# Layers 0 and 1 as one list of steps with two gates, and a new layout of layer 0's tensors

## Chip, cores and metric

The kernel runs on one core of a Trainium2 chip. The metric is the device time of one execution in microseconds (us); the median of a few runs is compared. Engines are named as in the profile: PE is TensorE (PEld its weight loads), DVE is VectorE, ACT is ScalarE, POOL is GpSimd, SP is SyncE, which here only issues DMAs.

## Reference

Four attention layers follow one another on 8 batches. Cut to the two that the change touches (layers 2 and 3, a grouped-query attention and an attention with a feed-forward part, fill the span from about 1400 us on):

```python
# layer 0: x [8,256,512], ctx [8,256,512], 16 heads of 16 channels, tokens along the last axis
q, k, v = Wq x + bq, Wk ctx + bk, Wv ctx + bv
attn = softmax(where(mask, (q/4)^T k, -inf))          # per head 512 x 512
mean, ex2 = attn v, attn v^2
std = sqrt(relu(ex2 - mean^2))
x = (instance_norm(x, mask) * std + mean) * mask
# layer 1: latents = x (256 of 512), 256 rows of ctx before them as keys, 16 heads of 32
h = concat(ctx, latents)                               # 512 tokens
q, k, v = latents q_w + q_b, h kv_w + kv_b
a = softmax(where(mask, q k^T / 32, -inf)) v
a = rmsnorm(a out_w + out_b + latents)
x = gelu(a mlp_w1 + mlp_b1) mlp_w2 + mlp_b2 + latents
```

Layer 1's batch b needs layer 0's output of batch b alone, which goes through a DRAM scratch (`x1`).

## The kernel before

Work is cut into 16 items: batch b and half h (8 heads each), item i = 2b + h. Each item goes through a chain of steps with names like `("0.smax", b, h, j)`. Each engine is given one list of steps and works through it strictly in that order; steps wait for each other through semaphores (`q.wait_ge(...)`). The lists come from the functions `layer0_order` to `layer3_order`, which give each step a position in beats: a position of 17.4 means that the step belongs 0.4 of a beat into beat 17. A beat is one item's time. Positions set the order alone: what a beat lasts comes out of the run. `order_of` (line 225) sorts each engine's list by position plus a small engine-dependent delay from `LATER` (line 211).

Layer 0, for item i: beat i+1 holds projections (`proj`), the split of q and k into three bf16 parts on ACT, DVE and POOL (`split`), their way through DRAM into stacked operands QS and KS (`stack`, SP), and `v`. Beat i+2 holds 32 score matmuls with a row maximum each on DVE (`smax`, L722 on PE and L1260 on DVE), then `rows` and `turn`, which write the negative maxima as further operand rows. Beat i+3 (from 0.25 on, reaching 0.64 into the next) holds 32 score matmuls (`sc`, L731) with an exponential on ACT each (L1050), `vals` (L741, the product with v), `fold` on POOL (L1563), `sums` (L749) and the copies `out` and `sout`. Beat i+4 holds the reciprocals of the sums (`fetch`, `inv`, `spread`, through DRAM) and for h = 1 the tail of the batch: `f1`, `f2`, `f3`, `f3b`, `sq`, `f4`, `f5`, of which the last stores x1.

Layer 1, for item i, positions from i on: `load` (latents and ctx^T, DMAs from POOL), the mask row (L1304, L1307, then `mrow` by SP into KX), `lat` (transposes, L617), `kproj` and `qproj` (2 each), `v` (4), `smax` (4 steps of 4 heads, PE L781 and L784, DVE L1319), `rows`, `turn`, `sc`, `vals`, `fold`, `sums`, and for h = 1 the output projection.

PSUM: ring A (banks 0 to 2) takes projections, v, layer 0's smax and turn; ring C (3 to 5) layer 0's sc; bank 6 vals; bank 7 layer 0's sums. Layer 1's smax and sc share one group, banks 3, 4, 5 and 7 (`GROUP`): each step refills all four as they are emptied.

The two layers meet as follows. `pipeline` (line 35) ends layer 0 with a barrier at beat 19. At a barrier all five engines wait until everything before it is done (DMAs counted up to a mark at 18). Then comes `1.start`: ACT issues the DMAs of four weights of 1024 KB each, SP two bias rows, POOL memsets KX, M3 and the ones. Then the tail of item 15 (fetch to f5) runs beside `load`, `lat`, `kproj`, `qproj` and `v` of layer 1's item 0. A second barrier follows, and after it `smax` of item 0 and the rest of layers 1, 2 and 3 in one sorted list. The barriers are there because the layers' tensors lie on the same SBUF addresses. From the second barrier on no all-engine barrier stands until the end; later overlaps are guarded by "gates" (`GATED`, line 235), at which only the engines named wait until what precedes a "mark" is done.

Of the kernel before, what the change touches and what calls it, by code (L numbers as in the profile page):

```python
# [16 lines left out]


def merge(*lists):

    placed = []
    for n, (steps, start, end) in enumerate(lists):
        for i, s in enumerate(steps):
            if s is not None and isinstance(s[0], float):
                placed.append((start + (end - start) * s[0], n, i, s[1]))
                continue
            s, delay = s if isinstance(s, tuple) and isinstance(s[1], float) else (s, 0.0)
            placed.append((start + (end - start) * (i + 0.5) / len(steps) + delay, n, i, s))
    return [(at, s) for at, _, _, s in sorted(placed, key=lambda x: x[:3]) if s is not None]


SPANS = ((0.0, 0.9), (0.0, 0.8), (0.05, 0.8), (0.0, 1.0), (0.0, 1.0))


def pipeline(stages, spans=SPANS, tail=None, keep=False, begin=()):


    n, order = len(ITEMS), []
    first = 0 if stages[0] else 1
    for i in range(first, n + 4):  # L40
        lists = []
        for s, (f, span) in enumerate(zip(stages, spans)):
            if f and 0 <= i - s < n:
                steps = f(*ITEMS[i - s])
                if steps:
                    lists.append((steps, *span))
        if i == n + 3 and keep:
            return order + [(i, ("barrier", 0, 0, 0))], lists[0]
        if i == n + 2 and keep:
            order.append((i, ("mark", -1, 0, 0)))  # L50
        if i == first and tail:
            order += [(i + at, st) for at, st in merge(*lists, (tail[0], 0.0, 0.8))]
            order += [(i + 1, ("barrier", 0, 0, 0))] + [(i + 1, st) for st in begin]
        else:
            order += [(i + at, st) for at, st in merge(*lists)]
    return order + [(n + 4, ("barrier", 0, 0, 0))], None
# [1911 lines left out]
```

## Time and profile before

| | |
|---|---|
| median of 3 runs | 3267.26 us (3261.61 to 3276.46) |
| profiled execution | 3280.75 us, span 3279.0 us |
| mean granted PE clock, profiled execution | 0.92 of full speed |
| busy share of the span: PE / DVE / ACT / POOL | 86% / 56% / 41% / 27% |
| layer 0 | start to about 690 us |
| weights and first projections of layer 1 | 690 to 747 us |
| layer 1, rest | 747 to about 1400 us |

In the rows below, times are us from the start of the span. The profile's page first shows busy time by engine, then the span in 40 slices of 82 us with the busy share in tenths. A row of the timeline has start, duration, engine, line, operation, output and inputs, and how many instructions were merged; in brackets stands how long the engine was idle before it and what ended that. "Landing" of a DMA is the time from its issue to its last byte.

### The profile page before, as it was taken

Reading aid. Unit: us, or ns where it says so; the run is one execution under the profiler, and the core shown is the slowest. Engines: PE = TensorE matmul, PEld = TensorE weight load, DVE = VectorE, ACT = ScalarE, POOL = GpSimd, SP = SyncE. Lnnn points to the kernel's source line nnn. Section 1 sums busy time; section 2 is a strip of 40 time slices with the busy share of each in tenths; the row PEclk is TensorE's granted clock in tenths of the full one; section 3 lists DMA queues with packets and bytes.
Section 4 is the critical chain, followed back from the end, with each engine's and each line's share of the span. In section 5 each row is a group of like instructions: output and inputs, shape, how many; then the busy total and the mean of one; then the engine's idle time right before and its main releaser. Section 6 shows DMA issues by size and latency. Waiting matters only on the chain. (4 is left out here: it accounts for less than half of the span.)

```text
span 3279.0 us, 41359 instructions
## 1 busy us (share of the span) xinstructions
PE 2819.3 (86%) x14624; PEld 1322.2 (40%) x14624; DVE 1838.1 (56%) x4498; ACT 1339.5 (41%) x2342; POOL 882.9 (27%) x722
## 2 busy tenths in 40 slices
PE   4999998858999999989999999986678888888895
PEld 1222222224555555556555545542223333233332
DVE  3777777713444433212555565567867676667641
ACT  0566666632333333322334333322215544554562
POOL 1677777742444444310010001001111010100000
PEclk7999999979999999899999999987678899999997
DMA  4444444220002000121323332333333232323210
GB/s 99 102 103 103 109 100 102 62 94 33 27 27 83 27 28 24 66 79 42 68 59 62 63 65 55 68 63 88 66 91 80 67 78 58 90 58 71 69 32 20
DMA packets 182335, 219.93 MB, mean 67 GB/s; under 512 B 40840, under 2 KB 135664, under 8 KB 175984
## 3 DMA queue, kind: packets, MB, share of 16 engines
q1 hardware_dynamic: 170064, 189.74, 25.2%
q0 software_dynamic: 6016, 20.98, 1.9%
q10 hardware_dynamic: 6048, 6.56, 0.6%
q8 instruction: 116, 1.90, 0.3%
q14 instruction: 91, 0.75, 0.1%
HBM read 146.90 MB, written 51.64 MB: 61 GB/s over the span
## 5 line engine op out<-in xcount | busy, mean ns | idle before, releaser
L1480 DVE TENSOR_REDUCE l_M<-PS 128x1 f32<-128x512 f32 x512 | 334.4, 682 | 136.9 <-PE PS L967 134.0
L1260 DVE TENSOR_REDUCE l_M<-PS 128x1 f32<-128x512 f32 x512 | 331.8, 683 | 139.6 <-PE PS L722 138.8
L1199 ACT ACTIVATE l_P<-PS 128x512 f32<-128x512 f32 x512 | 286.3, 599 | 252.9 <-PE PS L977 235.4
L1563 POOL TENSOR_TENSOR l_S<-l_P 128x512 f32<-128x512 f32 x256 | 327.2, 1311 | 67.4 <-ACT l_P L1050 67.4
L1050 ACT ACTIVATE l_P<-PS 128x512 f32<-128x512 f32 x512 | 278.4, 598 | 103.5 <-PE PS L731 101.7
L967 PE MATMUL PS<-l_KS,l_QS 97*128 97x512 bf16 x512 | 207.9, 417 | 99.5 <-DVE l_M L1480 68.6
L1319 DVE TENSOR_REDUCE l1a_M<-PS 128x1 f32<-128x512 f32 x256 | 158.8, 681 | 203.6 <-PE PS L784 203.6
L1164 ACT ACTIVATE l_P<-l_P 128x1024 f32<-128x1024 f32 x128 | 135.3, 1057 | 301.8 <-DVE l_P L1400 301.6
L1386 DVE CUSTOM_DVE_ANT_0 l_JK<-PS,l_MK 128x256 f32<-128x256 f32 x512 | 195.5, 419 | 104.9 <-PE PS L897 102.8
L612 PE MATMUL PS<-l_YT,l_w_mlp_w 128*128 128x256 f32 x1024 | 240.0, 391 | 5.2 <-ACT l_YT L1126 5.1
L722 PE MATMUL PS<-l_KS,l_QS 97*128 97x512 bf16 x512 | 202.9, 406 | 42.9 <-DMA l_KS<-l_MB 19.7
L862 PE MATMUL PS<-l_w_mlp_w,l_H 128*128 128x512 f32 x512 | 232.0, 601 | 0.9 <-DVE l_X L1367 0.9
L977 PE MATMUL PS<-l_QS,l_KS 100*128 100x512 bf16 x512 | 205.7, 411 | 29.9 <-ACT l_P L1199 29.7
L731 PE MATMUL PS<-l_QS,l_KS 100*128 100x512 bf16 x512 | 194.7, 395 | 28.7 <-ACT l_P L1050 21.3
L1596 POOL TENSOR_TENSOR l1a_S<-l1a_P 128x1024 f32<-128x1024 f32 x64 | 150.6, 2353 | 252.7 <-ACT l1a_P L1101 252.5
L1400 DVE TENSOR_TENSOR l_P<-PS,l_MKT 128x512 f32<-128x512 f32 x256 | 170.8, 683 | 77.0 <-PE PS L908 76.3
L612 PEld LDWEIGHTS PS<-l_YT,l_w_mlp_w 128*128 128x128 f32 x1024 | 198.7, 196 | 37.0 <-ACT l_YT L1126 6.1
L1653 POOL TENSOR_TENSOR l_T<-l_F,l_T 128x512 bf16<-128x512 f32 x32 | 37.0, 1155 | 628.4 <-DVE l_T L1468 628.4
L1101 ACT ACTIVATE l1a_P<-PS 128x512 f32<-128x512 f32 x256 | 132.2, 603 | 171.8 <-PE PS L808 171.8
L1624 POOL TENSOR_TENSOR l_T<-l_F,l_T 128x256 bf16<-128x256 f32 x32 | 21.4, 669 | 591.7 <-DVE l_T L1362 591.7
L967 PEld LDWEIGHTS PS<-l_KS,l_QS 97*128 97x128 bf16 x512 | 50.5, 101 | 271.0 <-DVE l_M L1480 149.9
L722 PEld LDWEIGHTS PS<-l_KS,l_QS 97*128 97x128 bf16 x512 | 50.8, 100 | 248.5 <-DVE l_M L1260 147.8
(244 smaller groups left out, 4758.6 us busy)
## 6 DMA issues: line engine op xcount, KB each, us to landing
l_QS<-q_scratch SPq DMA_DIRECT2D x128, 128.0 KB, 5.7
q_scratch<-l_T SPq DMA_DIRECT2D x96, 128.0 KB
l_QS<-q_scratch SPq DMA_DIRECT2D x32, 384.0 KB, 5.0
k_scratch<-l_T SPq DMA_DIRECT2D x96, 128.0 KB
l_KS<-k_scratch SPq DMA_DIRECT2D x32, 384.0 KB
l_QS<-q_scratch SPq DMA_DIRECT2D x32, 256.0 KB, 5.6
l_KS<-k_scratch SPq DMA_DIRECT2D x32, 256.0 KB
l_RB<-l_recs SPq DMA_DIRECT2D x32, 256.0 KB
```

The costliest lines, as they stand in the source:

```text
L612: x = q.e.matmul(o, l, r, start=(n == 0), stop=(n == len(pairs) - 1), skip_group_check=True, **kw)
L722: e.matmul(PS[:, bank, :], t.Q[i % 3][0:97, hd, qt * 128:qt * 128 + 128], t.K[i % 3][0:97, hd, :], start=True, stop=True).then_inc(q.sem(" ...
L731: e.matmul(PS[:, bank, :], t.K[i % 3][0:100, 4 * g + m, kt * 128:kt * 128 + 128], t.Q[i % 3][0:100, 4 * g + m, :], start=True, stop=True, ...
L862: x = e.matmul(PS[:, 7, :], t.H1[:, o, tt * 128:tt * 128 + 128], t.w2[:, o, :], start=(o == 0), stop=(o == 15), skip_group_check=True)
L967: e.matmul(PS[:, bank, :], t.Q[i % 3][0:97, hd, qt * 128:qt * 128 + 128], t.K[i % 3][0:97, hd, :], start=True, stop=True).then_inc(q.sem(" ...
L977: e.matmul(PS[:, bank, :], t.K[i % 3][0:100, hd, kt * 128:kt * 128 + 128], t.Q[i % 3][0:100, hd, :], start=True, stop=True, skip_group_che ...
L1050: e.activation(t.P[quad % 4][:, m, :], PS[:, COUNTS.bank[st], :], ACT.Exp, scale=0.25).then_inc(q.sem("act.exp", st), 1)
L1199: e.activation(t.P[quad % 4][:, m, :], PS[:, COUNTS.bank[st], :], ACT.Exp, scale=0.25).then_inc(q.sem("act.exp", st), 1)
L1260: e.tensor_reduce(t.M[i % 2][:, qt, hd:hd + 1], PS[:, COUNTS.bank[st], :], AX.X, ALU.max).then_inc(q.sem("dve.smax", st), 1)
L1386: x = e.tensor_tensor_reduce(out=t.JK[n][:, :], in0=PS[:, COUNTS.bank[st], 256 * n:256 * n + 256], in1=t.MK[:, qt, :], scale=1.0, scalar=- ...
L1480: e.tensor_reduce(t.M[i % 2][:, qt, hd:hd + 1], PS[:, COUNTS.bank[st], :], AX.X, ALU.max).then_inc(q.sem("dve.smax", st), 1)
L1563: x = e.tensor_tensor(t.S[j % 2][:, m, :], t.P[2 * j % 4][:, m, :], t.P[(2 * j + 1) % 4][:, m, :], ALU.add)
```

## The change

`merge` and `pipeline` are dropped. Layer 0's steps keep their positions, item 15's tail included, and all layers' steps go into one sorted list, layer 1's positions shifted by `BEGIN1 = 18.35`. Both barriers between the layers are gone. In their place:

- mark 3 at 17.4 and gate 3 at 17.6, for ACT, POOL and SP. Behind it, at 17.61, `1.start` now holds the k, q and v weights (ACT), the row vb (SP) and on DVE a memset that waits for that row. `load` of batch 0 stands at 17.65, `lat` at 18.35, `kproj` at 18.45 and 18.55, `qproj` at 18.65 and 18.72, `v` at 18.8 to 19.16.
- mark 4 at 19.4 and gate 4 at 19.6, for ACT, DVE, POOL and SP. Behind it `1.start2`: the out weight (ACT), the row ob (SP), DVE's second memset, POOL's memsets of KX, M3 and ones.
- layer 1's first `smax` steps stand at 19.81 to 20.11 (0.1 apart, before 0.2) and wait on PE for layer 0's last exponential and last `sout`. Item 1's kproj stands at 19.45 and 19.55, its qproj at 19.65 and 19.72, its v from 19.8.
- the mask's load and its arithmetic become a step of their own, `mload`, for each batch at -0.6 beats (before: load at -0.9, the arithmetic 0.1 later on DVE, `mrow` at -0.75); `load` moves to -0.7, `mrow` to -0.5. The arithmetic is one instruction in place of two.

Layer 0's tensors get other addresses, and some of layer 1's too, so that what layer 1 writes between the gates lies on nothing that layer 0 still uses. Shapes, types and instructions of layer 0 stay.

```diff
-    return pipeline((a0, a1, a2, c, p), ((0.0, 1.0),) * 5, keep=True)
+    order = [(2 * b + h + beat + at, st) for b, h in ITEMS for beat, part in enumerate((a0, a1, a2, c, p)) for at, st in part(b, h)]
+    return order + [(-9, ("0.start", 0, 0, 0)), (17.4, ("mark", 3, 0, 0)), (19.4, ("mark", 4, 0, 0))]
+BEGIN1 = 18.35
...
         if h == 0:
-            at = -0.9 if b else 0.0
-            out += [(at, k("load")), (at + 0.15, k("mrow"))] + [((0.6 + at) if b else 0.05, k("lat", 0)), ((0.7 + at) if b else 0.08, k("lat", 1))]
+            out += [(-0.9 if b > 1 else -0.7, k("load")), (-0.6 if b else 1.2, k("mload")), (-0.5 if b else 1.27, k("mrow"))]
+            out += [(-0.3 if b else 0.0, k("lat", 0)), (-0.2 if b else 0.03, k("lat", 1))]
...
-        out += [(1.05 + 0.2 * n, k("smax", n)) for n in range(4)] + [(1.8, k("rows")), (1.81, k("turn"))]
+        out += [((1.05 + 0.2 * n) if (b, h) > (0, 0) else (1.46 + 0.1 * n), k("smax", n)) for n in range(4)] + [(1.8, k("rows")), (1.81, k("turn"))]
...
+    order = [(2 * b + h + at, st) for b, h in ITEMS for at, st in steps(b, h)]
+    return order + [(-0.75, ("gate", 3, 0, 0)), (-0.74, ("1.start", 0, 0, 0)), (1.25, ("gate", 4, 0, 0)), (1.25, ("1.start2", 0, 0, 0)),
+                    (18.95, ("mark", 2, 0, 0))]
...
-GATED = {0: ("pe", "sp", "pool"), 1: ("pe", "sp"), 2: ("pe", "act", "dve", "pool", "sp")}
+GATED = {3: ("act", "pool", "sp"), 4: ("act", "dve", "pool", "sp"), 0: ("pe", "sp", "pool"), 1: ("pe", "sp"), 2: ("pe", "act", "dve", "pool", "sp")}
...
             elif kind == "1.smax":
-                q.wait_ge("pool.start", ("1.start", 0, 0, 0))
+                q.wait_ge("pool.start", ("1.start2", 0, 0, 0))
                 q.wait_ge("mrow", step("1.mrow", 2 * b))
                 q.wait_ge("act.k", step("1.kproj", i, g))
                 q.wait_ge("act.q", step("1.qproj", i, g))
+                q.wait_ge("act.exp", ("0.sc", B - 1, 1, 31))
+                q.wait_ge("act.sums", ("0.sout", B - 1, 1, 1))
...
             if kind == "1.start":
                 q.wait_ge("rows", st)
-                e.memset(t.MB[0][:, 256:512], 0.0)
+                e.memset(t.MB[0][:, 256:512], 0.0).then_inc(q.sem("dve.start", st), 1)
+            elif kind == "1.start2":
                 e.memset(t.MB[1][:, 256:512], 0.0).then_inc(q.sem("dve.start", st), 1)
-            elif kind == "1.load":
+            elif kind == "1.mload":
                 q.wait_ge("inm", st)
-                q.next_needs(e.tensor_scalar(t.MF[:, :], t.MI[:, :], 0.0, None, ALU.not_equal))
                 q.wait_ge("mrow", step("1.mrow", i - 4))
-                q.wait_ge("dve.start", ("1.start", 0, 0, 0))
-                e.tensor_scalar(t.MB[b % 2][:, 0:256], t.MF[:, :], -1.0, NEG, ALU.add, ALU.mult).then_inc(q.sem("dve.mask", st), 1)
+                q.wait_ge("dve.start", ("1.start2" if b else "1.start", 0, 0, 0))
+                e.tensor_scalar(t.MB[b % 2][:, 0:256], t.MI[:, :], 0.0, -NEG, ALU.is_equal, ALU.mult).then_inc(q.sem("dve.mask", st), 1)
```

## Rows read from the trace of the kernel before

**Rows 1.** Windows: length, busy PE, PEld, DVE, ACT, POOL, clock, DMA share, GB/s.
```profile
610.00:651.50 41.50, 39.25 (x234) 10.34 (x233) 28.82 (x56) 29.25 (x57) 31.26 (x31) 1.00 0.15 36
651.50:689.60 38.10, 28.68 (x152) 5.18 (x152) 7.94 (x7) 26.06 (x46) 34.01 (x26) 0.88 0.16 42
689.60:702.90 13.30, 0.00 (x0) 0.01 (x1) 0.00 (x0) 0.60 (x1) 4.28 (x14) 0.50 0.74 250
702.90:726.10 23.20, 22.32 (x72) 14.72 (x72) 4.49 (x16) 4.73 (x10) 0.92 (x4) 0.81 0.31 110
726.10:747.40 21.30, 0.00 (x0) 0.02 (x1) 7.14 (x7) 5.14 (x7) 8.78 (x6) 0.56 0.10 37
...
765.00:1400.00 635.00, 620.51 (x4775) 355.43 (x4776) 244.08 (x546) 215.91 (x447) 252.55 (x126) 0.98 0.12 39
```

**Rows 2.** Timeline of PE across the two barriers.
```profile
687.60 1.94 PE L749 MATMUL PS<-l_S,ones 128*32 128x512 f32 x8 [3.16 <-POOL l_S L1563]
702.92 1.94 PE L617 MATMUL PS<-ident,l1a_LAT 128*128 128x128 f32 x8 [13.38 <-DMA l1a_LAT<-x_scratch]
...
747.41 2.09 PE L781 MATMUL PS<-l1a_K,l1a_Q 32*128 32x512 f32 x8 [21.39 <-DMA x_scratch<-l_OUT]
...
764.87 1.14 PE L781 MATMUL PS<-l1a_K,l1a_Q 32*128 32x512 f32 x8
```

**Rows 3.** Timeline of PE in layer 1, back to back: v, lat (two), kproj.
```profile
770.08 1.99 PE L612 MATMUL PS<-l1a_w_v_w,l1a_HT 128*128 128x256 f32 x8
771.91 1.04 PE L617 MATMUL PS<-ident,l1a_LAT 128*128 128x128 f32 x8
...
781.42 3.70 PE L612 MATMUL PS<-l1a_HT,l1a_w_k_w 128*128 128x512 f32 x8
```

**Rows 4.** Timeline of PE in layer 0, back to back: one vals step, two score matmuls.
```profile
638.55 1.06 PE L741 MATMUL PS<-l_P,l_V 128*32 128x512 f32 x8
639.55 0.39 PE L722 MATMUL PS<-l_KS,l_QS 97*128 97x512 bf16 x1
639.78 0.38 PE L731 MATMUL PS<-l_QS,l_KS 100*128 100x512 bf16 x1
```

**Rows 5.** Waits of 651.5 to 690: who for whom, us, times, longest.
```profile
PE PS L731 <- ACT l_P L1050: 3.9, 4, 3.1
...
PE PS L749 <- POOL l_S L1563: 3.2, 1, 3.2
...
PE PS L731 <- DMA l_QS<-l_MT: 1.4, 1, 1.4
```

**Rows 6.** Timeline of SP, then of ACT, about position 17.6.
```profile
630.88 0.59 SPq L1721 DMA_DIRECT2D l_EX<-l_E  x1
...
633.19 1.08 ACT L1050 ACTIVATE l_P<-PS 128x512 f32<-128x512 f32 x2 [0.78 <-PE PS L731]
```

**Rows 7.** Waits of 690 to 765: DVE's for the bias rows.
```profile
DVE l1a_MB L1300 <- DMA l1a_row_ob<-in_rows: 31.0, 1, 31.0
```

**Rows 8.** DMA issues of 685 to 760: queue, count, KB each, median us to landing.
```profile
l1a_w_v_w<-in_v_w ACTq DMA_DIRECT2D x1, 1024.0 KB, 15.3
...
l1a_row_vb<-in_rows SPq DMA_DIRECT2D x1, 256.0 KB, 8.0
...
l1a_KX<-l1a_MB SPq DMA_DIRECT2D x8, 1.0 KB, 2.4
```

**Rows 9.** POOL's mask load, all of layer 1: issue to landing, and DVE's wait for it.
```profile
DMA to landing us min/median/max: 4.2/4.7/10.1
...
DVE l1a_MF L1304 <- DMA l1a_MI<-in_mask: 47.2, 6, 9.0
```

**Rows 10.** Timeline of POOL at `1.start`: first memset, first load issued.
```profile
691.35 0.21 POOL L1574 MEMSET l1a_ones<- 128x128 bf16 x1 [3.80 <-DMA l_sums<-l_SS]
...
693.63 0.94 POOL L1584 DMA_DIRECT2D l1a_LAT<-x_scratch  x1
```

**Rows 11.** Costliest groups of the page: layer 0's score matmuls with their maxima.
```profile
L722 PE MATMUL PS<-l_KS,l_QS 97*128 97x512 bf16 x512 | 202.9, 406 | 42.9 <-DMA l_KS<-l_MB 19.7
```

More of the change, by code:

```diff
@@ L14 @@
 NEG = 1e30
[L19 to L56, printed above, removed]
 def layer0_order():
@@ L114, in steps @@
         return out
-    order = sorted([(2 * b + h + at, st) for b, h in ITEMS for at, st in steps(b, h)] + merge((tail[0], 0.0, 0.8)), key=lambda x: x[0])
-    first = lambda x: x[0] < 1 or x[1][0][0] == "0"
-    order = [x for x in order if first(x)] + [(1, ("barrier", 0, 0, 0))] + [x for x in order if not first(x)]
-    return order + [(18.95, ("mark", 2, 0, 0))]
+    order = [(2 * b + h + at, st) for b, h in ITEMS for at, st in steps(b, h)]
+    return order + [(-0.75, ("gate", 3, 0, 0)), (-0.74, ("1.start", 0, 0, 0)), (1.25, ("gate", 4, 0, 0)), (1.25, ("1.start2", 0, 0, 0)),
+                    (18.95, ("mark", 2, 0, 0))]
 BEGIN2 = 16.75
@@ L183, in whole_order @@
 def whole_order():
-    o0, tail = layer0_order()
-    order = [(0, ("0.start", 0, 0, 0))] + o0 + [(0, ("1.start", 0, 0, 0))]
-    rest = [(BEGIN2 + at, st) for at, st in layer2_order()] + [(BEGIN2 + 18.3 + at, st) for at, st in layer3_order()]
-    o1 = layer1_order(tail)
-    n = o1.index((1, ("barrier", 0, 0, 0))) + 1
-    order += o1[:n] + sorted(o1[n:] + rest, key=lambda x: x[0])
+    places = ((0, layer0_order()), (BEGIN1, layer1_order()), (BEGIN1 + BEGIN2, layer2_order()),
+              (BEGIN1 + BEGIN2 + 18.3, layer3_order()))
+    order = sorted([(begin + at, st) for begin, steps in places for at, st in steps], key=lambda x: x[0])
     order += [(99, ("barrier", 0, 0, 0))]
@@ L249 @@
     "0.f3": ["dve.f3", "pool.f3", "act.f3y"], "0.f3b": ["dve.f3b"], "0.sq": ["act.sqrt"], "0.f4": ["dve.f4"], "0.f5": ["pool.f5"],
-    "1.start": ["dve.start", "pool.start"],
-    "1.load": ["dve.mask"], "1.lat": ["pe.lat", "act.lat"], "1.kproj": ["pe.proj", "act.k"], "1.qproj": ["pe.proj", "act.q"],
+    "1.start": ["dve.start"], "1.start2": ["dve.start", "pool.start"],
+    "1.mload": ["dve.mask"], "1.lat": ["pe.lat", "act.lat"], "1.kproj": ["pe.proj", "act.k"], "1.qproj": ["pe.proj", "act.q"],
     "1.v": ["pe.v", "dve.v"], "1.smax": ["pe.smax"] + 4 * ["dve.smax"], "1.rows": ["dve.rows"], "1.turn": ["pe.turn", "act.turn"],
@@ L343, in count @@
     def count(self, engine, order):
[L344 removed]
+        uses, total = {}, {}
         for st in order:
@@ L1130, in scalar2 @@
                 q.wait_ge("dve.v", ("1.v", B - 1, 1, 3))
-                q.wait_ge("dve.mask", ("1.load", B - 1, 0, 0))
+                q.wait_ge("dve.mask", ("1.mload", B - 1, 0, 0))
                 q.wait_ge("pstore", ("1.f2", B - 3, 1, 0))
@@ L1586, in gpsimd1 @@
                 e.dma_start(t.H[b % 2][:, :, 0:256], tokens(I["ctxT"][b])).then_inc(q.sem("inc", st), 16)
-                q.wait_ge("dve.mask", step("1.load", i - 2))
+            elif kind == "1.mload":
+                q.wait_ge("dve.mask", step("1.mload", i - 2))
                 e.dma_start(t.MI[:, :], I["mask1"][b:b + 1, :]).then_inc(q.sem("inm", st), 16)
@@ L1736, in sync1 @@
                 row(q, t.vb, "vb1")
+            elif kind == "1.start2":
                 row(q, t.ob, "ob1")
             elif kind == "1.mrow":
-                q.wait_ge("pool.start", ("1.start", 0, 0, 0))
+                q.wait_ge("pool.start", ("1.start2", 0, 0, 0))
                 q.wait_ge("pe.sc", step("1.sc", i - 3, 3))
-                q.wait_ge("dve.mask", step("1.load", i))
+                q.wait_ge("dve.mask", step("1.mload", i))
                 for m in range(4):
```

87 lines of the change are left out of this document (48 added, 39 removed), and 4 rows, old and new, of tables (LATER, MOVES).

## The prediction

> **What bounds the kernel now.** I read the slices of the page first: PE's busy share is at nine tenths from the second slice through layer 1, but for the two slices about 690 to 770 us, where its clock row dips too. So I cut that stretch into windows at the barriers [rows 1] and went through PE's timeline [rows 2]. The reader should see four things. Until 651.5 us PE is the bound of layer 0 (39.25 of 41.5 us). From 651.5 to 689.6, when only item 15's second pass is left, nothing is full: PE 28.68 of 38.1, ACT 26.06, POOL 34.01. Then PE stands still twice, 13.38 us for the first loads behind barrier one and 21.39 us for the last store of layer 0 before barrier two [rows 2], with its clock at 0.50 and 0.56, that is at the lower of its two levels. From 765 on PE is full again (620.5 of 635 us). Since PE is the bound on both sides and each engine's list is in order, the time saved is how much earlier PE stands at the same remaining work. I call work P what PE has done at 764.87, when it starts the third score step of item 0: all of layer 0, item 0's projections, two score steps, item 1's kproj, qproj and one v. From there everything shifts together.
>
> **The work of the overlap.** Warm costs, from rows back to back: a kproj 3.70, a v 1.99, both lat steps 1.04 [rows 3]; a qproj has v's shape. Item 0's projections are 1.04 + 2 x 3.70 + 2 x 1.99 + 4 x 1.99 = 20.4 us, 20.0 without the overlap of the rows. They took 22.3 us of PE before, at clock 0.81 [rows 1]. Item 1's two kproj: 7.3 us. They now stand in layer 0's last beats, between 18.35 and 19.55. What layer 0 itself gives PE between 651.5 and 689.6 is 9 vals and 6 sums steps at 1.00 (from 638.55 to 639.55) and 32 scores at 0.22 [rows 4]: 22 us. The step `sums` 3 is the last of them, so up to it PE has 21 + 20 + 7.3 = 48.3 us.
>
> How much of the 16 us of slack is really filled? The waits in that stretch are 3.9 us for ACT, 3.2 for the last fold, 1.4 for the maxima's DMA [rows 5], the rest is slow clock and short waits. Filled entirely the stretch takes 48.3 us; not filled at all, 38.1 + 27.3 = 65.4. POOL needs 34 us in it and ACT 26, both well under 48, so neither is the new bound; but PE still works in order, and scores come three at a time before ACT must empty a bank. I take 52, nearest to full.
>
> **Removed.** Both standstills, 13.4 + 21.3 us, and 2 us that the slow clock cost between 747 and 765 [rows 1, 2]. By themselves they are only gone if the things below don't put others in their place.
>
> **Gate 3 (17.6; ACT, POOL, SP).** Mark 3 includes SP's last `out` of item 13, issued until 631.5 us [rows 6]; with 2 to 2.4 us to land, as the small ones take [rows 8], it is done at 633.5 or so. ACT reaches 17.6 just behind its exponentials at 633.2 [rows 6]. Cost 0 to 3 us, taken as 0, since what follows covers it. Queued behind it on ACT are exponentials, on SP item 14's `out`.
>
> **The row vb (17.61; DVE).** This is the wait that the diff adds without naming it a gate. DVE's new memset stands at 17.61, amid item 15's row maxima, and waits for a DMA that SP issues only behind gate 3. Before, DVE sat in that place for 31.0 us with nothing queued [rows 7]; the row itself took 8.0 us to land beside the weights [rows 8]. Now 12 maxima are queued behind it, and PE can run on for three banks, about 1.5 us. So PE stalls 8.0 + 0.5 - 1.5 = 7 us. Bounds: 2.7 us, if it lands like the smallest load in 4.2 [rows 9]; 9, if in 10.1. The nearest row is the row's own 8.0. ACT's three DMA issues fall into the same stall and cost nothing more; the 3 MB of weights land 15.3 us after their issue [rows 8], at 649 of the old time, while the maxima's DMA and kproj come after 655 of it once the stall is added.
>
> The Trainium skill (DMA: Bandwidth & Descriptors, section Queues, rings and completion order) says that each DMA engine takes turns between the queues packet by packet. By that rule the 256 KB row should not queue behind 3 MB of another engine's queue; the row's 8.0 us [rows 8], longer than a mask behind 1 MB, sides with sharing but not with a free pass. At full priority the stall would be near its lower bound of 2.7 us and the saving 4 us larger.
>
> **Gate 4 (19.6; ACT, DVE, POOL, SP).** It waits for the last fold, `sums` 2 and the landing of the last `out`. After the last vals step `out` needs 0.6 us on ACT, eight issues of 0.6 each [rows 6] and 2.4 to land [rows 8]: 8 us. PE meanwhile has sums 2 and two kproj, 8.3 us, so the gate opens about when PE reaches sums 3 (call it G), and costs PE nothing by itself. What is late next is the mask: POOL's memsets take 2.3 us from the gate [rows 10], SP's four rows 4 x 0.64 = 2.6, their landing 2.4 [rows 8]: the first score step can start at G + 7.4. PE has sums 3, two qproj and a v, 6.8 us. Next DVE: `mload` of batch 1 (19.75) is issued by POOL after the memsets and two load issues, at G + 4.4, and lands 4.7 us later [rows 9]; DVE waits for it at 19.76, ahead of the maxima, so the first bank is free at G + 9.1 + 0.4 + 0.7 = G + 10.2, and the second score step ends at G + 11.6. That is 3.5 us of PE idle. If the load takes 10.1 as once [rows 9], it is 9.
>
> **Layer 0's tail.** Item 15's fetch, inv, spread and f3 to f5 now lie among score steps on DVE, ACT and POOL. Its four DMAs in a row through DRAM (put, fetch, rec, spread) take 2.4 to 4.2 us each [rows 8, 9], some 12 us; DVE has four score steps (10 us) before f3 at 20.2. Its waits hold back the shared score banks. I take 4 us, between 0 and 12 (the whole chain uncovered).
>
> **At nothing.** The mask arithmetic is 1 instruction instead of 2, hidden under PE. Layer 0's new addresses change no instruction; both ends of that are a rival below. The later `mload` puts DVE's wait straight behind POOL's issue: also a rival.
>
> **The sum.** G = 651.5 + 7 + 52 = 710.5. Work P is done at 710.5 + 11.6 = 722.1, against 764.9: 42.8 us. Less 4 for the tail, and 2 for slow clock after the stalls: 37 us. The profiled execution took 3280.75 us (span 3279.0, 1.75 around it) and would take 3244. It lies 13.5 us above the median of the runs, 3267.26; taken from the median, **3230 us**. The bounds: filling complete, row landing at once and tail covered add 4 + 4 + 4, to 49; overlap as bad as 60 us, 2 for the row, 5 for the mask, 8 for the tail take away 23, to 14. Own range of the likeliest case: 3218 to 3253.
>
> The clock supports it in a separate way: PE fell to the lower level (1.2 GHz) in both standstills and came back at 0.81 and higher [rows 1]. The Trainium skill (TensorE: Matmul & The Clock Gate, section What's actually happening) ties the level to recent activity. The row stall of 7 us is idle time of the same kind, so it would be paid for again by slow matmuls: the 2 us above would become about 4, by that rule; the trace's wait of 3.1 us on ACT with a mean clock of 0.88 in its window leaves both open.
>
> **Rivals.**
> (a) *The overlap is fuller than I think.* POOL and ACT have room, and 16 us of slack is what PE's work wants. With no row stall and 49 us, the saving is 49 to 57 us: 3214. Against it: the in-order DVE wait is written in the diff.
> (b) *The gates are barriers under another name.* If gate 3 drains the engines (13 us as at the first barrier [rows 2]) on top of the row and gate 4 costs 10 more, the saving is 37 - 23 = 14 us: 3253, no difference. For it: all DMA queues of SP are counted. Against it: marks stand 0.2 beats, some 6 us, ahead of the gates, as long as a DMA needs.
> (c) *Slower: DVE waits for the mask in every batch.* Place: `mload`, now at -0.6 on POOL and -0.59 on DVE; before DVE came 0.1 beat later than POOL. Price: DVE already waits 47.2 us in six batches for it, 9.0 at most [rows 9]. If those waits grew by a tenth of a beat, 3.5 us, and all of it, 9 + 3.5 us, held up PE in seven batches, that is 88 us less 37, so 3318. It decides from 37 / 7 = 5.3 us of PE per batch. Against it: PE is busy 620.5 of 635 us in spite of those 47 us [rows 1, 9]; the refill of the score group has the room. Likely 0 to 1 us per batch.
> (d) *The new addresses matter.* Layer 0 holds 512 score matmuls of 406 ns [rows 11]. Were each 3% slower, 6 us; nothing in the trace ties a duration to an address.
>
> **How the numbers follow.** Likeliest case 0.62; (a) 0.12; (b) 0.16, of which half stays faster by 16 us or more; (c) 0.06; (d) and others 0.04. A measurement of this kernel can tell about 0.5% (16 us) from no change. Faster: 0.60 + 0.12 + 0.09 = 0.81; same: 0.12; slower: 0.07. The range goes to (a) with its full price below and to (b) above: 3208 to 3256.
>
> **What would show it.** Right: PE without a gap over 5 us between 660 and 765; a DVE wait of 5 to 9 us at about 633 released by the row vb, with PE idle 5 to 7; PE's third score step of item 0 at 720 to 735; the chain behind gate 4 as ordered, a PE gap of 2 to 6 us. Wrong: ACT or SP idle over 5 us at 17.6; score matmuls of layer 0 over 410 ns; PE under 600 busy us in 635 in layer 1.

## The result, and the profile after

The kernel after took 3257.82 us (median of 20 runs), the kernel before 3275.59 us (20 runs). The ratio is 0.9953, 95% interval 0.9938 to 0.9968: 15 us faster by the ratio, 18 by the medians. That is a clear difference, but less than half of the 37 us forecast, and the 15 us are just inside what the prediction called no change. One of the 20 runs of the kernel after took 5403 us, far from all others (3250 to 3278), and is left out of the ratio. The profiled execution has a span of 3254.5 us (before 3279.0), a granted PE clock of 0.925 on average, PE busy 86%.

Windows of the kernel after. Columns as in [rows 1]; the bounds follow the same work: 656.5 is 5.0 us behind item 15's turn of layer 0 (before 651.5, 4.5 behind it), 713.1 the step `sums` 3, 733.0 the end of work P.

```profile
640.00:656.50 16.50, 14.35 (x79) 3.41 (x77) 7.02 (x15) 10.85 (x20) 10.61 (x9) 0.91 0.66 226
656.50:713.10 56.60, 51.10 (x232) 21.39 (x232) 13.51 (x18) 31.45 (x57) 35.36 (x31) 0.94 0.11 30
713.10:733.00 19.90, 13.20 (x57) 7.57 (x56) 3.29 (x8) 2.12 (x4) 4.07 (x14) 0.80 0.35 121
733.00:765.00 32.00, 30.57 (x188) 17.73 (x191) 18.99 (x34) 14.16 (x23) 10.39 (x8) 0.91 0.07 26
765.00:1400.00 635.00, 602.86 (x4641) 343.30 (x4635) 232.17 (x516) 217.78 (x443) 255.32 (x127) 0.97 0.12 39
```

Both standstills of [rows 2] are gone. Item 15's second pass and layer 1's first projections now share one stretch in which PE works 51.1 of 56.6 us. PE has done work P at 733.0, where the kernel before needed 764.87: a lead of 31.9 us. But the last line, against that of [rows 1], is not the same: PE has 602.9 busy us in 635, before 620.5. Part of that is only that the same window reaches other work at its end (a kernel that keeps its lead, the one counted from layer 1 below, has 614.6). The rest says that the lead was not kept.

PE's timeline about the overlap: the row stall, the last `sums`, the two qproj and a v, then the first score steps of layer 1. (The third score step itself starts at 736.7, behind a v that stood behind it before; work P counts up to 733.0.)

```profile
638.26 0.39 PE L692 MATMUL PS<-l_KS,l_QS 97*128 97x512 bf16 x1 [2.62 <-DVE l_M L1234]
...
713.13 1.07 PE L719 MATMUL PS<-l_S,ones 128*32 128x512 f32 x8
714.13 3.72 PE L582 MATMUL PS<-l1a_HT,l1a_w_q_w 128*128 128x256 f32 x16
717.69 1.89 PE L582 MATMUL PS<-l1a_w_v_w,l1a_HT 128*128 128x256 f32 x8
725.49 2.09 PE L753 MATMUL PS<-l1a_K,l1a_Q 32*128 32x512 f32 x8 [5.92 <-issue]
727.33 0.68 PE L756 MATMUL PS<-l1a_KX,l1a_ones 1*128 1x512 bf16 x4
728.79 3.01 PE L753 MATMUL PS<-l1a_K,l1a_Q 32*128 32x512 f32 x6 [0.79 <-DVE l1a_M L1293]
```

To see where a lead goes, take one event of each item, ACT's copy behind its `turn`, and subtract its times of two kernels. The lead, before minus after, is -4.5 us at item 15 of layer 0 (651.5 against 647.0: the row stall), then in layer 1 28.2 us at item 0, 22.0 at item 1, 14.7 at item 2, 12.5 at item 3, and 12.5 still at item 14. So 16 us were lost within three items, about 745 to 870 us, and nothing behind them up to item 14. Ahead of them, the 31.9 us at the end of work P had become 28.2 at item 0's turn; the same work, after and before:

```profile
733.00:747.10 14.10, 12.68 (x65) 8.07 (x68) 10.04 (x22) 1.22 (x3) 2.49 (x2) 0.80 0.06 20
```
```profile
764.90:775.30 10.40, 10.29 (x65) 6.86 (x64) 6.99 (x16) 1.08 (x2) 0.00 (x0) 1.00 0.00 0
```

PE needs 2.4 us more for 65 matmul records, at the lower clock behind its gap at 725, and waits 1.43 us for `rows`. Some 3 of these 3.7 us are lost as well in the kernel counted from layer 1 (below), which keeps the rest of the lead.

The wait that is new in the three items: first the waits of PE, 765 to 1400 us (us in all, times, longest), then three waits in PE's timeline, of which the first lies ahead of that window and belongs to item 0.

```profile
PE PS L764 <- DVE l1a_M L1303: 11.5, 3, 5.6
```
```profile
746.64 0.40 PE L764 MATMUL PS<-identb,l1a_M 128*128 128x128 bf16 x4 [1.43 <-DVE l1a_M L1303]
...
785.56 0.61 PE L764 MATMUL PS<-identb,l1a_M 128*128 128x128 bf16 x4 [5.61 <-DVE l1a_M L1303]
...
828.85 0.61 PE L764 MATMUL PS<-identb,l1a_M 128*128 128x128 bf16 x4 [5.29 <-DVE l1a_M L1303]
```

L764 is the step `turn`, which needs `rows` from DVE (L1300 to L1303). The same wait of the kernel before (its L792 for L1329) is 0.7 us, once, in the same window. DVE's timeline of the kernel after, then of the kernel before, both about `rows` of item 1; POOL's of the kernel after between them:

```profile
779.98 0.42 DVE L1285 TENSOR_TENSOR l1a_V<-PS,l1a_row_vb 128x256 f32<-128x256 f32 x1 [3.33 <-PE PS L582]
780.32 2.28 DVE L1300 TENSOR_SCALAR l1a_M<-l1a_M 128x16 bf16<-128x16 f32 x1
782.64 2.36 DVE L1301 SCALAR_TENSOR_TENSOR l1a_Mr<-l1a_M 128x16 f32<-128x16 f32 x1
785.03 0.20 DVE L1302 CAST l1a_M<-l1a_Mr 128x16 bf16<-128x16 f32 x1
785.27 0.23 DVE L1303 TENSOR_TENSOR l1a_M<-l1a_Mr,l1a_M 128x16 bf16<-128x16 f32 x1
```
```profile
780.21 2.34 POOL L1573 TENSOR_TENSOR l1a_S<-l1a_P 128x1024 f32<-128x1024 f32 x1 [5.37 <-ACT l1a_P L1075]
782.62 2.34 POOL L1577 TENSOR_TENSOR l1a_S<-l1a_S 128x1024 f32<-128x1024 f32 x1
```
```profile
804.28 0.41 DVE L1311 TENSOR_TENSOR l1a_V<-PS,l1a_row_vb 128x256 f32<-128x256 f32 x1
804.62 0.19 DVE L1326 TENSOR_SCALAR l1a_M<-l1a_M 128x16 bf16<-128x16 f32 x1
804.84 0.18 DVE L1327 SCALAR_TENSOR_TENSOR l1a_Mr<-l1a_M 128x16 f32<-128x16 f32 x1
805.06 0.20 DVE L1328 CAST l1a_M<-l1a_Mr 128x16 bf16<-128x16 f32 x1
805.30 0.23 DVE L1329 TENSOR_TENSOR l1a_M<-l1a_Mr,l1a_M 128x16 bf16<-128x16 f32 x1
808.03 0.42 DVE L1311 TENSOR_TENSOR l1a_V<-PS,l1a_row_vb 128x256 f32<-128x256 f32 x1 [2.50 <-PE PS L612]
```

Two things differ. Before, `rows` comes first and the last v of the next item (808.03) behind it; after, DVE does that v first, and it has to wait 3.33 us for PE. And since `rows` is now late, it meets POOL's last fold: two instructions of 0.19 and 0.18 us take 2.28 and 2.36, each ending when one of POOL's two additions ends.

Why did the order change, where the diff doesn't touch it? DVE's places are sorted. `rows` of item i stands at i + 1.8, with `LATER` 0.01 behind; `v` 3 of item i + 1 stands at i + 1 + 0.45 + 3 x 0.12. Both are i + 1.81, a tie. In floating point the tie is decided by rounding, and adding `BEGIN1` = 18.35 rounds anew:

```
item i   before: rows              v 3 of i+1          after: rows            v 3 of i+1
0        1.81                      1.81                20.160000000000004     20.16
1        2.8099999999999996        2.81                21.160000000000004     21.16
2        3.8099999999999996        3.81                22.160000000000004     22.16
3        4.81                      4.8100000000000005  23.160000000000004     23.160000000000004
```

Before, `rows` is smaller or comes first as the earlier step of two equal ones, for every item; after, it is larger for items 0, 1 and 2. The two large stalls are those of items 1 and 2. Item 0 has no fold of its own layer beside its `rows` yet, and its wait of 1.43 us doesn't come from the flip: it is 1.3 to 1.7 us in every kernel below that puts rows first again.

### The profile page after: what moved, and what is told of

Same layout as the page of the kernel before. It is cut to its first block and busy times, and to the rows that moved or that the text cites. A ratio compares the mean times of both kernels' runs of the same rounds, so it can differ in the third digit from the quotient of the medians.

```text
span 3254.5 us, 41335 instructions
## 1 busy us (share of the span) xinstructions
PE 2813.0 (86%) x14624; PEld 1318.5 (41%) x14624; DVE 1835.1 (56%) x4490; ACT 1345.0 (41%) x2344; POOL 881.4 (27%) x722
## 5 line engine op out<-in xcount | busy, mean ns | idle before, releaser
L692 PE MATMUL PS<-l_KS,l_QS 97*128 97x512 bf16 x512 | 203.7, 413 | 44.2 <-DVE l_M L1234 19.5
L939 PEld LDWEIGHTS PS<-l_KS,l_QS 97*128 97x128 bf16 x512 | 50.5, 101 | 276.2 <-DVE l_M L1455 152.2
L959 PE MATMUL PS<-l_P,l_V 128*17 128x512 f32 x1024 | 149.2, 657 | 0.9 <-ACT l_P L1173 0.9
```

The lines of the kernel that those rows point to most:

```text
L692: e.matmul(PS[:, bank, :], t.Q[i % 3][0:97, hd, qt * 128:qt * 128 + 128], t.K[i % 3][0:97, hd, :], start=True, stop=True).then_inc(q.sem(" ...
L939: e.matmul(PS[:, bank, :], t.Q[i % 3][0:97, hd, qt * 128:qt * 128 + 128], t.K[i % 3][0:97, hd, :], start=True, stop=True).then_inc(q.sem(" ...
```

## The experiments

Theory A: this tie costs the lost lead. Theory B: it is lost by something else of the change (contention with the late loads, the masks, the new addresses), and the order on DVE doesn't matter. Below, "counted from item 15's turn" means the time from ACT's copy behind that turn of layer 0 to the one behind item 14's of layer 1, taken from the profiled executions: before 670.5 us, after 653.5. It leaves out what layer 0 does.

**Rows first, in the kernel after.**

```diff
-... + [(1.8, k("rows")), (1.81, k("turn"))]
+... + [(1.799999, k("rows")), (1.81, k("turn"))]
```

> The changed kernel with one number altered: layer 1's rows step at 1.799999 beats in place of 1.8, so that on VectorE the rows step of items 0, 1 and 2 stands ahead of the fourth v of the next item again, as in the kernel before (one pair of Newton instructions of a later item changes places with a rows step too). Against the kernel before, the changed kernel is 31.9 us ahead when the third score step of item 0 starts, 28.2 at the turn of item 0, 22.0 at item 1's, 14.7 at item 2's, 12.5 at item 3's and at every one after. Theory A (the flipped order costs it): the two stalls of 5.6 and 5.3 us ahead of the turn and the one of 1.4 go, the lead at item 3's turn and at all later ones of layer 1 is 26 to 31 us, and the run is 10 to 17 us faster than the changed kernel, so 25 to 33 us faster than the kernel before. Theory B (the tail of layer 0 or the mask loads among layer 1's first steps cost it): the lead still falls to 12 to 16 us and the time stays that of the changed kernel.

Measured: 3241.86 us, ratio to before 0.9897 (0.9873 to 0.9921), 34 us faster; once more (below) 0.9881. PE waits for `rows` once, 1.4 us in all, at item 0 (753.2 us), and not at all between 765 and 1400 us:

```profile
PE PS L764 <- DVE l1a_M L1303: 1.4, 1, 1.4
```

The lead no longer shrinks: 21.7 us at item 0, 21.5 at item 14; 640.6 counted from item 15's turn. The lead is smaller than the 26 to 31 expected, and starts smaller than the 28.2, since this execution reached item 15's turn 3.9 us later and waited 4.2 us for the maxima (below).

**Last v first, in the kernel before.** The same flip of items 0 to 2, with nothing else of the change.

```diff
-out += [(0.45 + 0.12 * n, k("v", n)) for n in range(4)]
+out += [(0.45 + 0.12 * n - (1e-6 if n == 3 and 1 <= 2 * b + h <= 3 else 0), k("v", n)) for n in range(4)]
```

> The kernel before with the opposite edit: the fourth v of items 1, 2 and 3 stands a millionth of a beat ahead of the rows step of items 0, 1 and 2 on VectorE. Theory A: the same stalls appear in the kernel before, 5 to 6 us ahead of the turn for the items whose rows step meets a fold of GpSimd, 1 to 2 otherwise, and all later turns come 8 to 16 us later than in the kernel before; the run is 8 to 16 us slower. Theory B: no change within 3 us.

Measured: 3301.3 us, ratio 1.0075 (1.0048 to 1.0101), 25 us slower, more than the 8 to 16 expected. The waits of PE, 765 to 1400 us:

```profile
PE PS L792 <- DVE l1a_M L1329: 12.9, 4, 5.6
```

It is behind by 2.4, 8.4, 16.4 and 20.7 us at items 0 to 3, and no further; 1.2 of these it was behind at item 15's turn already, so counted from there it takes 690.0 us, 19.5 more than before. The two kernels' lists differ in three pairs of neighbours on DVE and in nothing on the other four engines, so no contention, mask or address of the change is in it. Theory A holds from both sides.

**No fold beside it.** In the kernel after the last fold's two additions of items 0 and 1 are memsets of the same tiles; those sums are left out of the result.

```diff
+quiet = i in (0, 1) and j == 3
-x = e.tensor_tensor(to[:, :, :], t.P[j][:, :, 0:256], t.P[j][:, :, 256:512], ALU.add)
+x = e.memset(to[:, :, :], 1.0) if quiet else e.tensor_tensor(...)
```

> The changed kernel, in which the two additions of the last fold of layer 1's items 0 and 1 on GpSimd are replaced by memsets of the same tiles, which read nothing; so the sums of these two items are left out. The order on VectorE stays as in the changed kernel. It tells the two parts of the stall apart. If the rows step's instructions are slow (2.3 and 2.4 us in place of 0.2) because GpSimd is adding at that time, they fall to about 0.2 us each and the stalls of 5.6 and 5.3 us ahead of the turns of items 1 and 2 fall to about 1.4 us, as at item 0. If the order alone makes the stalls, they stay above 5 us and the instructions stay slow.

Measured: one execution, 3250.84 us, 646.4 counted from item 15's turn. DVE's timeline of item 1, and POOL's:

```profile
783.16 0.42 DVE L1285 TENSOR_TENSOR l1a_V<-PS,l1a_row_vb 128x256 f32<-128x256 f32 x1 [3.33 <-PE PS L582]
783.50 0.87 DVE L1300 TENSOR_SCALAR l1a_M<-l1a_M 128x16 bf16<-128x16 f32 x1
784.41 0.18 DVE L1301 SCALAR_TENSOR_TENSOR l1a_Mr<-l1a_M 128x16 f32<-128x16 f32 x1
784.63 0.76 DVE L1302 CAST l1a_M<-l1a_Mr 128x16 bf16<-128x16 f32 x1
```
```profile
783.37 0.95 POOL L1574 MEMSET l1a_S<- 128x1024 f32 x1 [5.36 <-ACT l1a_P L1075]
784.38 0.95 POOL L1578 MEMSET l1a_S<- 128x1024 f32 x1
```

PE's longest wait for `rows` falls from 5.6 to 2.6 us, not to the 1.4 expected. What is left is the wait behind the v and the shorter hold by the memsets: 0.87 and 0.76 us in place of 0.19 and 0.20 are 1.2 us, and 2.6 less 1.2 is 1.4. The kernel after gives the same split: 2.28 and 2.36 us in place of 0.19 and 0.18 are 4.3 of its 5.6 us, and 1.3 are the order alone. The 2.28 us are no property of the DVE instruction: it lasts as long as POOL's instruction beside it (0.87 us in a memset of 0.95). The Trainium skill (SBUF — State Buffer, section SBUF: two separate sides) says that DVE and GpSimd share a pair of ports that is locked for a whole instruction, and that a DVE instruction with two SBUF inputs is held only by a GpSimd one that reads SBUF. The trace agrees: L1301 with its two inputs took 2.36 us beside the addition and 0.18 beside the memset, which reads nothing. L1300 and the cast L1302 have one input each and were held by the memset too; why, no run here shows.

**The row later.** DVE's `1.start` half a beat later, so that it doesn't wait for the row vb amid the maxima.

```diff
-("1.rows", "dve"): 0.01,
+("1.rows", "dve"): 0.01, ("1.start", "dve"): 0.5,
```

> The changed kernel with VectorE's small memset of 1.start placed half a beat later, behind the row maxima of layer 0's last item, so that its wait for the row vb holds back no maximum. If the stall of 2.6 us at 635 is that wait: TensorE has no wait over 0.5 us for VectorE between 630 and 650, and the turn of item 15 of layer 0 comes at 647 to 648 in place of 651.5; the lead at layer 1's later turns grows by 3 to 5 us. If the gate on ScalarE and the other transfers make the delay, the turn stays at 650 or later.

Measured: one execution, 3269.88 us. The stall at the row is gone, item 15's turn comes at 645.8 (after 651.5); but PE waits 5.4 us for the DMA of the maxima instead of 1.8:

```profile
654.33 1.03 PE L701 MATMUL PS<-l_QS,l_KS 100*128 100x512 bf16 x2 [5.37 <-DMA l_QS<-l_MT]
```

So the stall is taken away, but the wait behind it grew by 3.6 us (why, is seen in the next experiment), and its removal shows in no time of the whole kernel (one execution, with the tie of items 0 to 2 still in it).

**The masks earlier, and the weights later.** The first of the two is rows first, with the second bias row and the wo weight moved behind the mask rows of batch 0, the load of batch 1 moved behind the load of its mask, and that mask taken up 0.1 beat later on DVE; the second is the same, with the row and the three weights later too.

```diff
-out += [(-0.9 if b > 1 else -0.7, k("load")), ...
+out += [({0: -0.7, 1: -0.55}.get(b, -0.9), k("load")), ...
-("1.mload", "dve"): 0.01,
+("1.mload", "dve"): 0.11, ("1.start2", "act"): 0.6, ("1.start2", "sp"): 0.6,
+("1.start", "dve"): 0.5, ("1.start", "act"): 0.6,    # only in the second
```

> e1_rows_first with the transfers behind gate 4 in another order, so that the mask rows of layer 1's first score step come ahead of what is needed later: ScalarE issues the out weight and SP the row ob 0.6 beats later, GpSimd issues batch 1's mask ahead of batch 1's load, and VectorE takes up that mask 0.1 beats later. In the changed kernel TensorE waited 5.9 us ahead of that step (725.49) and VectorE 9.0 us for batch 1's mask. If the mask rows landed late because 2.25 MB were on the way ahead of them: they land within 4 us of the last issue, not 6.5, TensorE's wait falls to 2 to 3.5 us and the lead at layer 1's later turns grows by 3 to 6 us over e1_rows_first, measured from the turn of layer 0's item 15. If the landing time is that of the small transfers themselves, the wait stays above 5 us and nothing is gained.

> e5_mask_chain, and on top of it VectorE's memset with its wait for the row vb half a beat later (as in e4_row_late) and ScalarE's three weight loads 0.6 beats later, behind the DMA that carries item 15's negated maxima. In the changed kernel that DMA was waited for 1.8 us, in e4_row_late 5.4 and in e1_rows_first 4.2, with 3 MB of weights under way; before 1.4. If the weights slow it: the wait falls to 1.5 us or less, the stall of 2.6 to 3 us for the row is gone as well, and from the turn of item 15 to layer 1's later turns 3 to 6 us are gained over e5_mask_chain. If the weights then come too late, TensorE waits for them ahead of the first kproj (it has 6.6 us to land, and kproj stood 32 us behind its issue): a wait of 2 to 8 us there, and the gain is nothing.

Measured: 3242.56 us, ratio 0.9908 (0.9884 to 0.9932), and 3239.42 us, ratio 0.9890 (0.9868 to 0.9913). The four mask rows landed in 1.9 to 4.4 us, instead of 4.7 to 6.1 (rows first), so the larger loads had been slowing them. PE's wait ahead of layer 1's first score step went from 5.3 us (rows first) to 3.8 and 3.6, where 2 to 3.5 were expected:

```profile
723.74 2.09 PE L753 MATMUL PS<-l1a_K,l1a_Q 32*128 32x512 f32 x8 [3.78 <-issue]
```

The 1.5 us are there in the trace and too small for the times; counted from item 15's turn it is 636.3 and 638.8 us, against 640.6 and 637.5 with rows first. In the second the row stall is gone as well, yet the wait for the maxima is 4.2 us, where 1.5 or less was expected. That wait was 4.2 and 1.1 us in two executions of one and the same kernel (rows first), so single executions differ. What goes with it in all of the traces is where the three weights are when ACT copies item 15's maxima. In ten of the 14 profiled executions none is under way (in the kernels with the change the last has landed 1.1 to 3.2 us earlier), and PE goes on 4.0 to 5.0 us behind that copy. In the other four it is 7.4 to 11.1 us. In two of these (rows first, the row later) the last weight lands 1.9 and 2.7 us behind the copy, and a DMA of 16 KB, which SP waits for before it issues the maxima, takes 4.5 and 3.3 us instead of 1.7 to 2.2. With rows first:

```profile
SPq L1704 <- DMA l_recs<-l_l0r: 4.0, 1, 4.0
```

In the other two (weights later, overlap later) the weights are issued from 0.4 us ahead of the copy to 3.0 behind it, and the maxima travel beside them. So the delay that was meant to free the maxima from the weights put the two side by side. No run moves the weights alone, so this is read from the traces and not tried.

**The overlap half a beat later.** Rows first, with `BEGIN1 = 18.85`.

> e1_rows_first with BEGIN1 = 18.85 in place of 18.35: all of layer 1 and what follows stands half a beat later against layer 0, gates 3 and 4 with it, so that about half of item 0's projections no longer fall into the last pass of layer 0. If the lead comes from TensorE's slack in that pass (9.4 us idle and a clock of 0.88 from 651.5 to 689.6, and a standstill until the projections begin), 6 to 12 us of it are lost: the lead at layer 1's turns falls from e1's by that much. If removing the two standstills alone made the lead, it stays within 3 us of e1's, since the list still has no barrier.

Measured: 3249.07 us, ratio 0.9919 (0.9896 to 0.9942); 644.1 counted from item 15's turn, against 640.6 and 637.5 with 18.35. Some 3.5 to 6.6 us are lost, between the 6 to 12 expected of PE's slack and the 3 of the other reading; in the times the intervals overlap. Here PE waits 5.5 us for the maxima, beside the weights, which may well be the loss. Later is no better.

**Counted from layer 1.** Instead of shifting one step by hand, the kernel after with zero put at the start of layer 1. Every tie of layers 1 to 3 falls as before.

```diff
-places = ((0, layer0_order()), (BEGIN1, layer1_order()), (BEGIN1 + BEGIN2, layer2_order()),
-          (BEGIN1 + BEGIN2 + 18.3, layer3_order()))
+places = ((-BEGIN1, layer0_order()), (0, layer1_order()), (BEGIN2, layer2_order()),
+          (BEGIN2 + 18.3, layer3_order()))
```

> The kernel after, with all places counted from the start of layer 1 instead of from layer 0 (layer 0 at -18.35, layer 1 at 0). Every tie of layers 1 to 3 then falls as in the kernel before; some ties of layer 0 fall otherwise. Theory (the tie of rows and v 3 is the whole cause of the lost lead): as with rows put first by hand, PE waits for DVE's turn rows under 2 us in all, and the lead at item 14's turn, from item 15's turn of layer 0, is 29 to 31 us against before; ratio to before 0.988 to 0.992. Side question, layers 2 and 3: the kernel after gained another 10 us there with nothing changed in the code. If ties of layers 2 and 3 do that, this kernel gains 0 to 2 there, and its ratio is about 0.993. If it is no matter of ties, it gains 8 to 12 there like the others.

Measured: 3246.68 us, ratio 0.9898 (0.987 to 0.9926); 637.3 counted from item 15's turn, once more (below) 634.3. PE's wait for `rows` between 765 and 1400 us is 0.2 us. Item 0's is still there, so it isn't the tie's, and DVE's `rows` of item 1 is back at its short form:

```profile
743.99 0.40 PE L764 MATMUL PS<-identb,l1a_M 128*128 128x128 bf16 x4 [1.43 <-DVE l1a_M L1303]
```

```profile
773.92 0.19 DVE L1300 TENSOR_SCALAR l1a_M<-l1a_M 128x16 bf16<-128x16 f32 x1
774.15 0.18 DVE L1301 SCALAR_TENSOR_TENSOR l1a_Mr<-l1a_M 128x16 f32<-128x16 f32 x1
```

**Do ties matter in layers 2 and 3?** The kernel after was also 11.6 us shorter than the kernel before from item 14's turn to the last turn of layer 3, in code that the change doesn't touch, but for ties there that fall otherwise too. Four runs asked whether they are the cause: the kernel before with new ties there, twice, rows first once more, and the one counted from layer 1 once more. The first two also have `rows` at 1.799999, so that the ties of layer 1's rows stay as before, a line that the diff below doesn't show.

```diff
-rest = [(BEGIN2 + at, st) for at, st in layer2_order()] + [(BEGIN2 + 18.3 + at, st) for at, st in layer3_order()]
+rest = [(18.35 + BEGIN2 + at, st) for at, st in layer2_order()] + [(18.35 + BEGIN2 + 18.3 + at, st) for at, st in layer3_order()]
-order += o1[:n] + sorted(o1[n:] + rest, key=lambda x: x[0])
+order += o1[:n] + sorted([(18.35 + at, st) for at, st in o1[n:]] + rest, key=lambda x: x[0])
```

> The kernel before, with 18.35 added to every place behind the second barrier, so that the ties of layers 2 and 3 fall as in the kernel after, and rows put at 1.799999, so that those of layer 1's rows stay as before. If ties of layers 2 and 3 are worth the 10 us that the kernel after gained there: 10 us less than before, ratio 0.997, with the lead growing between items 4 and 18 of layer 2. If not: the same as before, ratio 1.000 within 0.002, lead within 3 us up to layer 2's first item.

> The kernel after with rows put first by hand, once more, as the measure for the other two on the same chip: ratio 0.988 to 0.992; a gain of 8 to 12 us in layers 2 and 3 if that gain belongs to the kernel, another number if it belongs to the single execution.

> The kernel after counted from the start of layer 1, once more and in more rounds. Side question, layers 2 and 3 alone: in single executions the kernels with the ties of before gained 0 to 4 us there against the kernel before, nearly all with the new ties 8 to 16. If those ties are worth some 10 us, this kernel gains again under 5 us from item 14's turn to the end, at a ratio of 0.990 or 0.991. If the gain belongs to single executions, it may be anything, and the ratio is 0.988 to 0.989 like the one with rows first by hand.

> The kernel before with the ties of layers 2 and 3 as in the kernel after, once more and in more rounds. If those ties are worth some 10 us: 8 to 16 us gained from item 14's turn to the end, ratio 0.996 to 0.998 with 1 outside the interval. If not: ratio 0.999 to 1.001.

Measured: the kernel before with new ties 0.998 (0.9958 to 1.0003) and 0.9995 (0.9979 to 1.0011); rows first 0.9881 (0.985 to 0.9913); counted from layer 1 0.9926 (0.9906 to 0.9946). Over that stretch, the kernel before with new ties was 16.2 us shorter than the kernel before in one execution and 4.6 longer in the next. A single execution of one kernel moves by 20 us there, so neither the 11.6 us nor a part of it is shown to belong to the change. The one counted from layer 1, with the old ties, gained 3.8 and 4.9 us there, which is inside that scatter. In the times, rows first lies at 0.988 to 0.990 and the one counted from layer 1 at 0.990 to 0.993 (0.9926 is outside what it was expected to be either way): the ties of layers 2 and 3 may be worth 0.2%, or nothing.

## Why the prediction was right and wrong

**The step that failed** is the first one: "From there everything shifts together." A lead of 31.9 us was there at work P, 28.2 at item 0's turn, and 12.5 three items on, because a sorted list with a tie in it is not moved unchanged by adding a constant. The sum had no term for an order that changes in steps that the diff doesn't name. Without that flip the kernel runs at 0.9897, 0.9881, 0.9898 and 0.9926 of before, some 32 us faster on average; the forecast of 37 us in 3280.75 is 0.9887. So the price of the tie is about 17 us of 3275 (0.9953 against a mean of 0.9901), some four fifths of the miss in the ratio; counted from item 15's turn it is 16.1 us (653.5 against a mean of 637.4 over the four executions without the flip). The last fifth is in terms that were mis-sized, below. The median that the prediction started from (3267.26) was also 8 us below the later one of 20 runs (3275.59); of the 28 us between 3230 and 3257.8, 8 are that, and 20 are the ratio (0.9946 between the medians in place of 0.9886).

**Both standstills removed**: right. 34.7 us of idle PE are gone, and [rows 2] has no counterpart but the 5.92 us at 725.49.

**Gate 3 at nothing**: right. ACT was idle 1.84 us ahead of its weights, with PE as the reason, and SP issued the row at 633.48, for which the prediction had 633.5.

**The row vb**: the mechanism was right, its size only in part. DVE waited for it in the middle of the maxima and PE with it, but 2.62 us instead of 7. What was off is the choice of the nearest row: 8.0 us [rows 8] was taken behind the weights' transfers; now SP issues the row 0.9 us ahead of them (633.48 against ACT's 634.35), and it landed in 3.9. DVE's wait:

```profile
637.50 0.17 DVE L1274 MEMSET l1a_MB<- 1x128 uint32 x1 [3.75 <-DMA l1a_row_vb<-in_rows]
```

The lower bound of 2.7 us was the right end for the stall (by the prediction's own sum, 4.2 + 0.5 - 1.5, it is 3.2). Where the row is issued behind a weight it is slow again: with the overlap later SP issued it 2.1 us behind the first weight, and it took 8.0 us to land. But the stall was not its whole price. PE worked slower behind it:

```profile
638.30:643.10 4.80, 4.80 (x20) 1.27 (x20) 4.04 (x7) 1.79 (x3) 0.85 (x1) 0.64 1.00 383
```

From item 14's turn of layer 0 to item 15's it takes 28.6 us before, 33.0 after: 2.6 of stall, and some 1.7 at a granted clock of 0.64 for 4.8 us (an estimate: 4.8 x 0.36). Over the seven executions with the row in this place (all but the two with it later and the one with the overlap later) the step takes 31.8 to 35.3 us, so the row costs 3.3 to 6.8, and the 7 us of the prediction lie just beyond that. Its sentence that such idle time is paid for again by slow matmuls was right.

**The overlap**: 57 us from the stretch's start to `sums` 3, where 52 was taken and 48.3 was full. PE was busy 51.1 of 56.6 us at clock 0.94; the 5.5 us idle are six short waits for ACT of 0.6 to 1.4 us. (The 1.8 us for the maxima's DMA end where the stretch starts; before, its 1.4 us lie inside.) `sums` 3 came at 713.1, not 710.5: the overlap cost 4.6 us more than the term, of which 2.0 came back from the row (5.0 where 7 was taken).

**Gate 4**: the chain was as ordered, its end later. From `sums` 3 to the end of work P it took 19.9 us against 11.6, the largest mis-sized term. POOL's first memset came 1.5 us after `sums` 3, SP's four rows at 717.0 to 719.5 as worked out, but they landed in 4.6 to 6.5 us instead of 2.4, beside three larger loads, the last at about 725.4. That made the 5.92 us of PE idle (3.5 said). The load of the next mask lasted 6.8 us, from its issue at 718.42 to DVE at 725.22:

```profile
725.22 0.28 DVE L1281 TENSOR_SCALAR l1a_MB<-l1a_MI 1x256 bf16<-1x256 int32 x1 [8.99 <-DMA l1a_MI<-in_mask]
```

The prediction had DVE's wait for it as the last link. It wasn't: DVE was through with it before PE began, and waited another 2.2 us for PE's first scores. The score steps ran at the lower clock, 2.09 and 3.01 us for eight and six matmuls with 1.14 for eight in [rows 2]. In all PE was idle 6.7 of the 19.9 us and busy 13.2, at a granted clock of 0.80. The prediction took off 4 for the tail and 2 for clock; 42.8 - 6 = 37, where 31.9 was measured. The miss up to there is 5 us: 2.6 by `sums` 3, 8.3 behind it, less the 6. PE's waits of 730 to 800 us show none for the tail of layer 0, so the 4 us for it stood for clock and landing times instead; that is luck. Another 3.7 us went up to item 0's turn.

**Rivals.** (a) A fuller overlap: no. (Its saving of 49 to 57 us was added up too high: 37 + 7 + 3 is 47.) (b) Gates that drain: they didn't; the time fell near that rival's 3253 for a different reason. (c) DVE waiting for the mask in every batch: refuted. The waits of DVE, 625 to 1400 us, have it twice, both about the gates, and less than the 47.2 us of [rows 9]:

```profile
DVE l1a_MB L1281 <- DMA l1a_MI<-in_mask: 18.4, 2, 9.4
```

(d) The addresses: layer 0's score matmuls took 413 ns against 406 [rows 11], beyond the 410 that was named as a sign of being wrong. But the sign doesn't tell the layouts apart: they took 406 to 413 ns in the ten executions with the new addresses and 406 to 411 in the four with the old ones. And item 15's turn came 4.5 us late by the row and the clock behind it: with the new addresses and the weights and row later it takes 28.6 us from item 14's turn, as before. So nothing of it is seen to be the addresses':

```profile
L692 PE MATMUL PS<-l_KS,l_QS 97*128 97x512 bf16 x512 | 203.7, 413 | 44.2 <-DVE l_M L1234 19.5
```

None of the rivals was the one that came.

**The clock.** After the two stalls of 5.6 and 5.3 us PE stayed slower than the idle time alone would say. Windows of the kernel after, then of the one with rows first, over the same work of items 1 and 2:

```profile
785.00:829.00 44.00, 38.16 (x302) 21.51 (x303) 16.83 (x28) 13.44 (x27) 15.97 (x9) 0.93 0.10 32
829.00:873.00 44.00, 44.00 (x310) 23.31 (x309) 16.81 (x39) 13.35 (x29) 11.68 (x5) 0.94 0.02 7
```
```profile
786.00:822.00 36.00, 35.99 (x302) 20.84 (x301) 12.47 (x26) 13.31 (x28) 16.04 (x9) 1.00 0.11 39
822.00:864.00 42.00, 42.00 (x313) 22.97 (x312) 17.02 (x40) 14.12 (x31) 16.39 (x7) 1.00 0.03 8
```

PE's busy time for 302 matmul records is 38.16 us against 35.99, and for the next item 44.00 against 42.00, at clocks of 0.93 and 0.94 against 1.00. So the two stalls, 10.9 us, cost about 4 more behind them. That makes 15 of the 15.7 us that the lead went down by (28.2 us at item 0's turn, 12.5 at item 3's).

## What to carry to other kernels

Where an order comes out of sorted places, look for ties before a constant is added to them, and compare each engine's list before and after for steps that the change doesn't name; a place that must come first needs a margin, not a rounding. Then follow the lead event by event through the part that is "unchanged": it shows in which item a gain is lost, which no sum over the changed stretch can. A small DVE instruction on the critical path belongs where POOL has no long one beside it.

## What the runs showed of the hardware that was not expected

- A DVE instruction of 0.2 us lasted 2.28 and 2.36 us beside a POOL addition of 2.34 us, and 0.87 us beside a memset of 0.95: it ends when POOL's ends. Two such in a row, each meeting another POOL instruction, make 4.6 us of 0.4.
- A row of 256 KB landed in 3.9 us when issued 0.9 us ahead of 3 MB on another queue (3.4 to 4.1 over the runs with it in this place), and in 8.0 when issued 0.8 us [rows 8] or 2.1 us (overlap later) behind the first weight of 1 MB.
- A stall of PE of 2.1 to 3.3 us in the middle of layer 0's last maxima cost 3.3 to 6.8 us in all, since the granted clock fell to the lower of its two levels behind it (0.64 on average over 638.3 to 643.1 us in the kernel after).
- Rows of 1 KB took 4.6 to 6.5 us to land beside larger loads in the kernel after, and 1.9 to 4.4 with those loads issued behind them; before, their median was 2.4 [rows 8].
- The wait for one small DMA (the maxima's) was 0.8 to 1.8 us in ten executions in which no weight of 1 MB was under way beside it or ahead of it, and 4.2 to 5.5 us in the four in which one was. Two of them are of one kernel, with 1.1 and 4.2 us.
